# Window attention and a ConvNeXt block: the low part of an exponential on GpSimd, one instruction for two

## The reference

```
# layer 0: attention in windows of 7 x 7, 12 heads of 16, fake-quantized (fq)
qkv = fq(xw) @ fq(Wqkv).T + bqkv               # xw: 1024 windows x 49 tokens x 192
q, k, v = fq(q * SCALE), fq(k), fq(v)
attn = fq(fq(q k^T) + bias)                    # bias from a table of relative positions
attn = softmax(attn, axis=3)
out = fq(attn v) @ fq(Wout).T + bout
# layer 1: depthwise 7 x 7 convolution, layernorm over channels,
#          192 -> 768 -> gelu -> response norm -> 192, and the residual
```

## Time and profile before

| | us |
|---|---|
| median of 3 runs | 5035.73 |
| lowest and highest of them | 5033.76, 5056.87 |
| the profiled execution | 5049.51 |
| its span, first to last instruction | 5047.8 |
| busy: PE, DVE, ACT, POOL | 4034.7, 3893.2, 3248.6, 1485.4 |
| attention stage (window 1290 to 2455) | 1165 |
| mean granted TensorE clock, whole span; attention stage | 0.901; 0.96 |

### The profile page before, as it was taken

One profiled execution on the slowest core, in us unless ns is written; L12 is line 12 of the kernel. 1 busy time (PEld: TensorE's weight loads), 2 busy tenths in 40 slices (PEclk: granted clock), 3 DMA queues, 4 the chain that ended last, 5 costly groups with the idle time before them and its releaser, 6 DMA issues. The chain is left out here.

```text
span 5047.8 us, 116742 instructions
## 1 busy us (share of the span) xinstructions
PE 4034.7 (80%) x40394; PEld 2558.1 (51%) x40394; DVE 3893.2 (77%) x7098; ACT 3248.6 (64%) x5602; POOL 1485.4 (29%) x1812
## 2 busy tenths in 40 slices
PE   1686777676698988988566669996689999999999
PEld 1233554444577777777455434443345454554544
DVE  7797999999999999989655410002799999999985
ACT  0675777775698988989466544443656666666664
POOL 0201111111667666766522200001132222212210
PEclk9997777876899999999777779997799999999999
DMA  8773666665333333333277778885122222222212
GB/s 319 208 216 106 161 160 164 166 165 133 81 96 95 91 95 92 95 87 99 83 274 268 274 250 289 288 288 177 47 73 95 74 90 82 74 93 83 90 56 68
DMA packets 270448, 725.18 MB, mean 144 GB/s; under 512 B 30602, under 2 KB 177290, under 8 KB 252362
## 3 DMA queue, kind: packets, MB, share of 16 engines
q1 hardware_dynamic: 259466, 675.31, 45.2%
q0 software_dynamic: 10560, 44.53, 2.2%
HBM read 428.25 MB, written 291.50 MB: 143 GB/s over the span
## 5 line engine op out<-in xcount | busy, mean ns | idle before, releaser
L861 POOL TENSOR_TENSOR exp_lo<-exp,exp_hi 128x294 f16<-128x294 f32 x1024 | 788.6, 798 | 358.1 <-ACT exp_hi L932 354.4
L1646 PE MATMUL out_psum<-gelu_hi,w_parts 128*128 128x448 f16 x2016 | 605.1, 355 | 58.7 <-DVE w_parts L1822 31.5
L1682 ACT ACTIVATE gelu_pair<-h_psum,b_rows,w_unscale 128x448 f32<-128x448 f32 x448 | 324.6, 728 | 413.1 <-PE h_psum L1598 224.9
L1718 DVE BATCH_NORM_STATS2 ln_stats<-z_img 128x6 f32<-128x192 f32 x448 | 126.0, 344 | 562.4 <-DMA z_img<-zd 561.7
L1382 PE MATMUL conv_psum<-c_in,toeplitz 128*128 128x448 f16 (+1 forms) x2304 | 470.2, 366 | 64.9 <-DMA dwb<-in_L_conv_dw_b_dram 62.4
L1598 PE MATMUL h_psum<-ln_parts_T,w_hi 128*128 128x448 f16 x2016 | 494.8, 355 | 17.5 <-DVE w_in L1781 15.7
L957 DVE SCALAR_TENSOR_TENSOR logit_int<-attn_int,scalars,bias_products 128x588 f16<-128x588 int8 x512 | 486.6, 951 | 13.1 <-issue 9.8
L1646 PE MATMUL out_psum<-gelu_lo,w_parts 128*128 128x448 f16 x1344 | 475.5, 354 | 0.0
L938 ACT ACTIVATE attn_int<-p_psum,scalars 128x588 int8<-128x588 f32 x512 | 386.3, 755 | 133.1 <-PE p_psum L464 131.2
L619 PE MATMUL range_psum<-q_diag,k_diag 128*128 128x196 bf16 x1536 | 275.6, 316 | 227.7 <-DVE p_min L701 224.9
L911 PE MATMUL o_psum<-a_v,exp_hi 128*128 128x34 f16 x6144 | 383.1, 179 | 77.9 <-DVE a_o L984 58.0
(11 more groups left out here) (313 smaller groups left out, 9879.9 us busy)
## 6 DMA issues: line engine op xcount, KB each, us to landing
k_diag<-kd SPq DMA_DIRECT2D x128, 384.0 KB, 5.1
toeplitz<-gd SPq DMA_DIRECT2D x48, 1024.0 KB, 17.1
yd<-y_out SPq DMA_DIRECT2D x16, 2880.0 KB, 27.2
c_in<-yd SPq DMA_DIRECT2D x24, 1920.0 KB, 9.4
zd<-c_out POOLq DMA_DIRECT2D x24, 1792.0 KB, 13.8
z_img<-zd SPq DMA_DIRECT2D x16, 2688.0 KB, 9.4
x_chunk<-in_x_dram SPq DMA_DIRECT2D x12, 3136.0 KB, 10.9
x_img<-in_x_dram SPq DMA_DIRECT2D x16, 2352.0 KB, 15.9
```

Source lines behind the costliest of these rows:

```text
L861: last = nc.gpsimd.tensor_tensor(el[r][:, :, 2 * a, 0:N], src[:, :, a], eh[r][:, :, 2 * a, 0:N], ALU.subtract)
L1646: last = nc.tensor.matmul(po[:, t, 0:TCH], w, hx[:, f, cols], start=f == 0 and x == 0, stop=f == NF - 1 and x == len(steps) - 1)
L1682: nc.scalar.activation(h[y // 2 % 3][:, y % 2], ph[:, y % 3, 0:TCH], ACT.Gelu, scale=k1[:], bias=b1[:, f:f + 1]).then_inc(hd, 1)
```

## The change

GpSimd's loop over the two halves a = 0 and 1 in L861, of 294 elements (6 x 49) each, becomes one instruction of 588 elements. Its outputs and second input step over the fields 0 and 2 (`0:3:2`), its first input is all of `exp`. The semaphore `lod` is raised once a step as before. The values are the same.

```diff
@@ -857,9 +857,7 @@
                     if stage(LAG_E + 4):
                         pool.wait_ge(pvd, m - 3)
                     src = e[r % 2][:].rearrange("p (a b n) -> p b a n", a=2, b=6)
-                    for a in range(2):
-                        last = nc.gpsimd.tensor_tensor(el[r][:, :, 2 * a, 0:N], src[:, :, a], eh[r][:, :, 2 * a, 0:N], ALU.subtract)
-                    last.then_inc(lod, 1)
+                    nc.gpsimd.tensor_tensor(el[r][:, :, 0:3:2, 0:N], src, eh[r][:, :, 0:3:2, 0:N], ALU.subtract).then_inc(lod, 1)
```

## The result

The changed kernel takes **5090.0 us** (three runs, 5085.7 to 5101.9), the kernel before 5035.7 (5033.8 to 5056.9). The ratio is 1.0082, with a 95% interval of 1.0052 to 1.0112: slower by 0.8%, where no change was forecast and the range ended at 5066. In a later session the same pair gave 1.0073 (1.0052 to 1.0094).

The account below looks back on a forecast made before the run. The prediction took VectorE's L957, blocked while GpSimd reads SBUF in the attention stage, as the bound. Its terms of -16 and +16 us summed to 0 on the median 5035.7, so 5036 us, range 5006 to 5066.

Parts of the forecast that it names:

- What bounds the kernel: Attention stage: VectorE is busiest, 1087 of 1165 us; GpSimd's reads block L957 and lengthen VectorE's period one for one.
- First term: GpSimd's subtraction: the single 588-element instruction takes 1.30 us, against 1.42 for the pair.
- R: Time from GpSimd's start until its reads end and L957 gets data: 1.22 us before, forecast 1.10 after.
- rival 1: GpSimd's merged instruction: its three-dimensional pattern runs slower than its rows; from 1.45 us length, +27 us, time 5063; chance 0.08.
- Second and third term: L957: shorter block in 395 steps, -16 us; lost gap between halves makes 117 free steps pay 0.133 each, +16 us.
- chain law: Attention stage, steady steps: x = 0.70 + 2b, so L957's block b = (R - 0.70)/3, 0.173 us before, 0.133 after.
- x: How long after GpSimd's start L957 starts; its block is R - x, none if x is over R.
- Rival 2: Unit ends and loop turns: after a stall L957 waits up to 1.10 us; 32 ends, +31 us, time 5067; chance 0.12.
- Rival 3: Attention stage: L957 starts before GpSimd, which is held instead; up to -67 us, time 4969; chance 0.14.
- The signs named ahead: Changed profile: L860 median 1.30 us, L957 mean near 950 ns, usually 0.93 to 0.98, distance 3.16, stage 1165 us.

Follow-up runs that it names:

- e3: Changed kernel with GpSimd subtracting one element a step in place of 588, all waits kept; 5008.3 us, ratio 0.9885 to the kernel before.
- e1: Changed kernel with the running maximum at a unit's end made a reduction of one SBUF input; 5058.2 us, ratio 0.9999 to the kernel before.
- e5: Changed kernel with one-input maximum, GpSimd waiting for VectorE's negative maximum, product with v one step later, eight exp_hi and exp_lo buffers; 5053.8 us, ratio 1.0007.
- e7: e5 with GpSimd also waiting for ScalarE's products, a 1x1 instruction before the subtraction, and later waits for filled buffers; 5011.8 us, ratio 0.9922.

## Why the prediction was wrong, point by point

- **What bounds the kernel.** Right. VectorE's L957 is stretched while GpSimd reads, and its period grows with it; e3, which removes the reading, gains 52 to 58 us.
- **First term, the length.** Right: 1.273 us in the median against 1.30, and R = 1.08 against 1.10. The third dimension of the pattern costs nothing, so rival 1 falls.
- **Second and third term, -16 and +16 us.** Nearly right in their sum. e1, in which only they act, stands at 0.9999 of the kernel before. L955's mean is 11 ns or 5.6 us over that of before, where the sum said 0. How large each of the two is was not measured apart.
- **The chain law** is right for the mean and wrong for the single step. It took all blocks to be equal. But x is 0.70 plus the two blocks on the way, so only the sum of three neighbouring blocks is fixed, at R - 0.70: 0.38 us in the changed kernel, 0.52 before, where the prediction's own rows have blocks of 0, 0.27, 0.24 and 0. The changed kernel, VectorE and then GpSimd:

```profile
2001.83 0.82 DVE L955 SCALAR_TENSOR_TENSOR logit_int<-attn_int,scalars,bias_products 128x588 f16<-128x588 int8 x1
2003.76 0.82 DVE L955 SCALAR_TENSOR_TENSOR logit_int<-attn_int,scalars,bias_products 128x588 f16<-128x588 int8 x1
2005.69 1.20 DVE L955 SCALAR_TENSOR_TENSOR logit_int<-attn_int,scalars,bias_products 128x588 f16<-128x588 int8 x1
2008.00 0.82 DVE L955 SCALAR_TENSOR_TENSOR logit_int<-attn_int,scalars,bias_products 128x588 f16<-128x588 int8 x1
...
2004.98 1.29 POOL L860 TENSOR_TENSOR exp_lo<-exp,exp_hi 128x588 f16<-128x588 f32 x1 [1.03 <-ACT exp_hi L930]
```

Two steps run free and the third pays 0.38. A third of that is the mean block that the law gives. Of the 510 sums of three in the stage 248 lie within 0.04 of 0.38 (before, 250 within 0.04 of 0.52).

- **The step that failed** is the claim behind them, that the change acts on L957 alone and that the chain law covers the stage. It was the steady law applied at the unit ends, with a second instruction of two SBUF inputs left out of the list of those that can be held. The prediction read the durations of L957 and L861 and stopped there. Had it asked of each VectorE line of the stage whether its record is stretched, L974 would have shown 273 ns for 16 elements; with the new hold of 1.08 us in place of 0.54, 32 instructions held by up to 1.08 us are up to 35 us, and each leaves the next L957 near GpSimd's start.
- **Rival 2** had the right places and half of the mechanism: 0.97 us at each of 32 unit ends, 31 us. Measured were 35.3 us there (20.9 + 14.4), 1.10 at each. But it put them down to L957 alone, not to the small instruction that comes first. It got 0.12, with the argument that a long block makes the next two steps free. They are free, since GpSimd then idles 2.14 us and starts late as well, but a free step is worth the usual block of 0.13 and no more, while the unit end has just cost the small instruction's 0.95 (1.17 less 0.22) and 0.83 for L955.
- **Rival 3**, VectorE first, did not come about by itself. With the whole subtraction in it, L957's mean fell under 0.90 only with the added wait of e5 and e7.
- **The signs named ahead.** L860's median and R came as said, and so did the distance from L955 to the GpSimd start behind the second next, 3.15 from 2001.83 to 2004.98. L955's usual value did not: 273 of 512 are under 0.84 us and 16 lie between 0.93 and 0.98, where few were to be at 0.82. The stage did not stay at its 1165 us, and that was the sign that mattered. L955's mean stayed under the 1.00 that was named as the mark for being wrong, at 0.990. The mark was set on one line, and 21 us passed beside it.

## What to carry to other kernels

Merging two short instructions on GpSimd into one also merges their holds on the second SBUF reader. Before doing so, list every VectorE instruction with two SBUF inputs in that stretch, the tiny ones too, and look at where each starts against GpSimd; a 16-element instruction cost up to 1.26 us here, and giving it one input cost nothing. Where both engines repeat in a fixed period, try tying GpSimd's start to just behind VectorE's two-input instruction, with buffers deep enough for the later result. It pays if the reads end before VectorE's next one begins: here the single long instruction fitted and the pair did not.

## What the runs showed of the hardware

- Which engine bears a meeting is settled by some tens of ns: 0.02 us ahead, GpSimd cost L957 1.07 us (1.89 against 0.82); 0.16 us behind, it cost VectorE nothing.
- An instruction that comes while GpSimd works off a backlog can be held through several of its instructions: one L962 of e7 was held through three, 4.47 us.
- A VectorE reduction of 32 elements over one SBUF input took 187 ns beside GpSimd's reads; the TENSOR_TENSOR of 16 and 16 that it replaced took 926 on average. That one-input instructions are not held is also what the Trainium skill says ("SBUF — State Buffer", "Who interferes with whom"); these runs agree.
- GpSimd's two-input subtraction took 193 ns for 1 element, 1008 for 444 and 1273 for 588, that is 1.84 ns an element on top of 0.19. The 2.6 cycles (2.17 ns) of the Trainium skill's "GPSIMD Engine Reference", section 3.1, are too many here.
